# Two attention chunks per FFN group: the factor chain in one unit, the second chunk one unit up, gate work behind the output additions, one table preload

## Chip, cores, metric

One core of one Trainium2 chip runs the whole kernel. The metric is the time of one execution on the device in microseconds; the value for the kernel before is the median of three runs.

## What is computed

Two sequences of 1,024 tokens, 512 features, fp32. A gated linear attention with a state of 64 x 128, added to its input, then a ternary gated FFN, added again:

```python
x = L0_attn_x                                   # (2, 1024, 512)
x = x + attn(layernorm(x))
x = x + ffn(layernorm(x))

# attn: q,k (K=64), v (V=128) from projections
beta  = sigmoid(x @ Wb + bb);  delta = softplus(x @ Wd + bd)
S = beta_t[:, None] * S + delta_t[:, None] * outer(k_t, v_t)     # a scan over t
o_t = q_t @ S;   result = o @ Wo

# ffn: w1, w2 (1408 x 512), w3 (512 x 1408), quantised
quant(w) = clip(round(w / (mean(|w|) + 1e-8)), -1, 1)
hidden = sigmoid(x @ quant(w1).T) * (x @ quant(w2).T)
result = hidden @ quant(w3).T
```

## The kernel before

Each engine has its own program, in an order written out by hand; semaphores join them. Nothing is reordered: an instruction that waits holds everything behind it on its engine.

**Chunks.** The scan is cut into C = 8 chunks of 128 tokens, both sequences together. A first part of the kernel (up to about 74 us) loads everything, projects all chunks, and carries attention through for chunks 0 and 1. Gates (beta, delta and the key factor) are made there for chunks 0 to 3; those of chunks 4 to 7 come later, by `exps(c)` on ScalarE (L532 to L535: Abs, Exp, Exp, Ln), `gates(c)` on VectorE (L700 to L702) and `gates(c)` on GpSimd (L399 to L407).

**Attention of one chunk** (`attn(s, c)` on each engine, s is a stage): `fetch` on GpSimd (L418 to L423) spreads factors, 21 small operations; `chain0` and `chain1` on VectorE are the seven products of a chain (L741), 4 and 3 of them; `levels` on TensorE (L954 to L959) is 28 + 4 + 1 small fp32 matmuls that need the chain; `gt` on ScalarE (L569) copies one result; `masks` on VectorE (L766, L771) puts the scores together; `o` on TensorE (L967 to L973) needs the masks; `state` on VectorE (L777), `oT` on ScalarE (L574); `wo` on TensorE (L984), four matmuls; `resid` on VectorE (L784) adds to x; `norm2` (L679 on VectorE, L380 to L386 on GpSimd); `apply` (L796); `xhi` on ScalarE (L581), `xlo` on VectorE (L802) and GpSimd (L444) split the normed x in two fp16 parts; `turn_x` on SyncE's queue (L305) transposes them by DMA into `xT`.

**FFN.** G = 4 groups of two chunks, 512 tokens each. A group has UNITS = 15 units: units 0 to 10 each make one of the HT = 11 hidden tiles with 16 fp16 matmuls (L1058: eight for the gate, eight for the up product), units 11 to 14 are the DT = 4 down units of 22 matmuls (L1072). Behind unit u of the first kind come the sigmoid on ScalarE (L645), the product hid on VectorE (L870), its high part on ScalarE (L651) and low part on VectorE (L875). Behind a down unit comes the output addition y on VectorE (L886), then a store. Three PSUM banks rotate, so a matmul group n waits for the reader of group n - 3; the first two of a group of the FFN wait for the output additions y(2) and y(3) of the group before:

```python
if m < 0:
    if n < 2 and g > 0:
        pe.wait_ge(y_ready, g * DT - 1 + n)
```

**Where attention lies in the FFN.** In group g < 3 the two chunks 2g + 2 and 2g + 3 are computed between the units, by the tables `PE_AFTER`, `DVE_AFTER`, `ACT_AFTER`, `POOL_AFTER`: each stage has a pair, the unit for the first and for the second chunk. On VectorE stages come behind hid and the low part of a unit u < 11 and ahead of y in a unit u >= 11. Group 3 has no attention. In group 0 the weights are also made ternary: `round12`, `round3` on VectorE (L728, L735; tables `R12_AT`, `R3_AT`), `sign12`, `sign3` on ScalarE (L553, L562; `W12_AT`, `W3_AT`), and a DMA transpose of each tile on SyncE's queue (L311, L320), which also carries x's transposes and the stores, in order, with three slots each for the signed tiles. `EXPS_AT` and `GATES_AT` say behind which (group, unit) the late gates are made. ScalarE's sigmoid needs another function table than Exp and Ln.

Of the kernel before, what the change touches and what calls it, by code (L numbers as in the profile page):

```python
# [16 lines left out]
def build_gated_delta_ternary_ffn(nc, x, Wq, Wk, Wv, Wo, Wb, bb, Wd, bd, w1, w2, w3, out):  # L17
# [8 lines left out]
    G = C // 2  # L26
# [19 lines left out]
    with ctx:  # L46
# [17 lines left out]
        wo = sb("wo", [P, D])  # L64
# [31 lines left out]
        oT = sb("oT", [P, B, P])  # L96
# [60 lines left out]
        def kept(c, a, b):  # L157
            return store[:, c, a * P:b * P]
# [58 lines left out]
        def sums_at(which):  # L217
# [1 line left out]

        UNITS = HT + DT  # L220

        PE_AFTER = {"levels": (2, 8), "o": (4, 10), "wo": (5, 11)}
        DVE_AFTER = {"chain0": (0, 6), "chain1": (1, 7), "masks": (2, 8), "state": (4, 10),
                     "resid": (5, 11), "norm2": (5, 11), "apply": (6, 12), "xlo": (7, 13)}
        ACT_AFTER = {"gt": (2, 8), "oT": (4, 10), "xhi": (7, 12)}
        POOL_AFTER = {"fetch": (0, 3), "norm2": (6, 12), "xlo": (7, 13)}

        W12_FRONT = 3
        W12_AT = {0: (3, 4), 1: (5, 6), 2: (7, 8), 3: (9, 10)}
        W3_AT = {4: (0, 1), 5: (2, 3), 6: (4,), 8: (5, 6), 9: (7, 8), 10: (9, 10)}  # L230
        R12_AT = {0: (7, 8), 1: (9, 10)}
        R3_AT = {2: (0, 1), 3: (2, 3), 5: (4,), 6: (5,), 7: (6, 7)}
        EXPS_AT = {(0, 11): (4, 5), (0, 13): (6,), (1, 11): (7,)}
        GATES_AT = {(0, 12): (4,), (0, 13): (5,), (0, 14): (6,), (1, 11): (7,)}
        R3_CUT = (0, 5 * P, H)

        def stages(after, u):

            return [(s, k) for s in after for k in range(2) if after[s][k] == u]
# [110 lines left out]
        def _(pool):  # L350
# [77 lines left out]
            def norm2(c):  # L428
                pool.wait_ge(stats2_ready, c + 1)
                rstd(c, C + c, mv2, rs2, XS).then_inc(rstd2_ready, 1)  # L430
# [9 lines left out]
            def xlo(c):  # L440
                if c > 0:
                    pool.wait_ge(xT_in, 16 * B * c)
                pool.wait_ge(xhi_ready, B * c + 1)
                nc.gpsimd.tensor_tensor(xs[:, 0, 1, :], xn2[:, 0, :], xs[:, 0, 0, :],  # L444
                                        ALU.subtract).then_inc(xlo0_ready, 1)
# [28 lines left out]
            for g in range(1, G - 1):  # L474
                fetch(2 * g + 2)
                if g == 1:
                    gates(5)
                    gates(6)
                fetch(2 * g + 3)
                norm2(2 * g + 2)  # L480
                xlo(2 * g + 2)
                if g == 1:
                    gates(7)
                norm2(2 * g + 3)
                xlo(2 * g + 3)

        @block.scalar
        def _(act):
# [38 lines left out]
            def exps(c):  # L527
                s = scratch(c)
                act.wait_ge(z_copied, c + 1)
                if c > 1:  # L530
                    act.wait_ge(stored, c - 1)
                nc.scalar.activation(s.z_abs, kept(c, 2, 3), ACT.Abs, bias=bias[:, 1:2])  # L532
                link(nc.scalar.activation(s.e_b, kept(c, 3, 4), ACT.Exp, scale=-1.0, bias=bias[:, 0:1]))
                link(nc.scalar.activation(s.e_d, s.z_abs, ACT.Exp, scale=-1.0))
                nc.scalar.activation(s.z_ln, s.e_d, ACT.Ln, bias=ones[:, 0:1]).then_inc(z_ready, 1)  # L535
# [30 lines left out]
            def attn(s, c):  # L566
                if s == "gt":
                    act.wait_ge(levels_done, c + 1)
                    nc.scalar.activation(GT[:, :], gt_at, ACT.Copy).then_inc(gt_ready, 1)  # L569
                if s == "oT":  # L570
                    act.wait_ge(o_done, c + 1)
                    if c > 0:
                        act.wait_ge(attn_done, c)
                    nc.scalar.activation(oT[:, :, :], oc[:, :].rearrange("p (b n) -> p b n", b=B)[:, :, 0:P],  # L574
                                         ACT.Copy).then_inc(oT_ready, 1)
                if s == "xhi":
                    if c > 0:
                        act.wait_ge(xT_in, 16 * B * c)
                    for b in range(B):
                        act.wait_ge(xn2_ready, B * c + b + 1)  # L580
                        nc.scalar.activation(xs[:, b, 0, :], xn2[:, b, :], ACT.Copy).then_inc(xhi_ready, 1)  # L581
# [57 lines left out]
            def group(g):  # L639
                for u in range(UNITS):  # L640
                    if u < HT:
                        act.wait_ge(gate_done, g * HT + u + 1)
                        if g * HT + u > 1:
                            act.wait_ge(hid_ready, g * HT + u - 1)
                        nc.scalar.activation(sig[:, u % 2, :], bank[2 * u % 3][:, :], ACT.Sigmoid,  # L645
                                             scale=1.0 / XS).then_inc(sig_ready, 1)
                    if 1 <= u <= HT:
                        act.wait_ge(hid_ready, g * HT + u)
                        if u == 1 and g > 0:
                            act.wait_ge(down_done, g * DT)  # L650
                        nc.scalar.activation(hid[:, 0, u - 1, :], hid32[:, (u - 1) % 2, :],  # L651
                                             ACT.Copy).then_inc(hi_ready, 1)
                    for c in EXPS_AT.get((g, u), ()):
                        exps(c)
                    if g == 0:
                        for j in W12_AT.get(u, ()):
                            sign12(j)
                        for j in W3_AT.get(u, ()):
                            sign3(j)
                    if g < G - 1:  # L660
                        for s, k in stages(ACT_AFTER, u):
                            attn(s, 2 * g + 2 + k)

            for g in range(G):
                group(g)
# [2 lines left out]
        def _(dve):  # L668
# [28 lines left out]
            def gates(c):  # L697
                s = scratch(c)
                dve.wait_ge(z_ready, c + 1)
                nc.vector.tensor_scalar(s.u_1, s.e_d, 1.0, -1.0, ALU.add, ALU.add).then_inc(u_ready, 1)  # L700
                link(nc.vector.tensor_scalar(s.e_b, s.e_b, 1.0, None, ALU.add))
                nc.vector.reciprocal(kept(c, 3, 4), s.e_b).then_inc(beta_ready, 1)  # L702
# [159 lines left out]
            def group(g):  # L862
                for u in range(UNITS):
                    if u < HT:
                        dve.wait_ge(up_done, g * HT + u + 1)
                        dve.wait_ge(sig_ready, g * HT + u + 1)
                        if g * HT + u > 1:
                            dve.wait_ge(hi_ready, g * HT + u - 1)
                            dve.wait_ge(lo_ready, g * HT + u - 1)
                        nc.vector.scalar_tensor_tensor(hid32[:, u % 2, :], bank[(2 * u + 1) % 3][:, :],  # L870
                                                       HS / XS, sig[:, u % 2, :], ALU.mult,
                                                       ALU.mult).then_inc(hid_ready, 1)
                    if 1 <= u <= HT:
                        dve.wait_ge(hi_ready, g * HT + u)
                        nc.vector.tensor_tensor(hid[:, 1, u - 1, :], hid32[:, (u - 1) % 2, :],  # L875
                                                hid[:, 0, u - 1, :], ALU.subtract).then_inc(lo_ready, 1)
                    if u >= HT and g < G - 1:
                        for s, k in stages(DVE_AFTER, u):
                            attn(s, 2 * g + 2 + k)
                    for c in GATES_AT.get((g, u), ()):  # L880
                        gates(c)
                    if u >= HT:
                        m = u - HT
                        dve.wait_ge(down_done, g * DT + m + 1)
                        y = tile(2 * g + m // 2, m % 2)
                        nc.vector.scalar_tensor_tensor(y, bank[(2 * HT + m) % 3][:, :], 1.0 / HS, y, ALU.mult,  # L886
                                                       ALU.add).then_inc(y_ready, 1)
                    if u < HT and g < G - 1:
                        for s, k in stages(DVE_AFTER, u):
                            attn(s, 2 * g + 2 + k)  # L890
                    if g == 0:
                        for j in R12_AT.get(u, ()):
                            round12(j)
                        if u == 2:
                            steps(1)
                        for k in R3_AT.get(u, ()):
                            round3(k)
# [213 lines left out]
```

## Time and profile before

| | |
|---|---|
| median of 3 runs | 346.62 us (346.48 to 348.51) |
| the profiled execution | 346.52 us |
| its span, first to last instruction | 344.8 us |
| TensorE busy | 331.6 us |
| VectorE, ScalarE, GpSimd busy | 206.4, 148.4, 104.3 us |
| granted TensorE clock | 1.00 throughout |
| FFN of group 0, 1, 2, 3 begins at | 74.0, 144.4, 215.8, 284.4 us |

Times in the trace count from the span's first instruction. A matmul's shown duration overlaps with its successors', so busy and idle times of TensorE are to be read beside the starts. In a timeline row an "x16" is that many instructions merged, and the bracket gives the idle time of the engine ahead of the first and what ended it.

### The profile page before, as it was taken

The numbers are of one execution on the slowest core, as the hardware profiler recorded it, in microseconds if no ns is written. First come the engines' busy times: TensorE is split into PE (matmuls) and PEld (weight loads), VectorE is DVE, ScalarE is ACT, GpSimd is POOL, SyncE is SP. The second block draws the span as 40 slices with busy tenths as digits, with TensorE's granted clock in tenths as the row PEclk, the third lists the DMA queues.
The fourth block names the chain that finished last, engine by engine and source line by source line (L and its number), as shares of the span: only waits on it lengthen the run. The fifth ranks groups of instructions, "written<-read, shape, count | busy, mean of one in ns | idle before, by whom it ended". The sixth has DMA issues, their size and how long they took to land.

```text
span 344.8 us, 5204 instructions
## 1 busy us (share of the span) xinstructions
PE 331.6 (96%) x1826; PEld 184.1 (53%) x1826; DVE 206.4 (60%) x454; ACT 148.4 (43%) x276; POOL 104.3 (30%) x350
## 2 busy tenths in 40 slices
PE   8899999998999999989999999999999999999996
PEld 6788878864544544435445444455454444444442
DVE  3678999299959836467388454473884433242311
ACT  1588687789745484522332512123332011323200
POOL 5797545495004003991032027200210110000000
PEclk9999999999999999999999999999999999999999
DMA  8999600457540720500003004100030040000011
GB/s 234 353 390 403 239 0 2 93 96 139 104 92 16 108 46 30 124 31 2 0 0 63 0 25 117 43 1 3 0 62 2 30 122 32 0 0 3 0 61 61
DMA packets 45658, 26.94 MB, mean 78 GB/s; under 512 B 37568, under 2 KB 38080, under 8 KB 45632
## 3 DMA queue, kind: packets, MB, share of 16 engines
q1 hardware_dynamic: 45632, 26.62, 28.2%
q8 instruction: 14, 0.23, 0.3%
q14 instruction: 12, 0.10, 0.1%
HBM read 13.89 MB, written 4.19 MB: 52 GB/s over the span
## 4 chain that ended last, share of the span: by engine, by line
PE 63%; DVE 16%; POOL 9%; issue 6%; ACT 3%; DMA 2%; SPq 1%; DVEq 0%; POOLq 0%; ACTq 0%
PE ffn L1058 34%; PE ffn L1072 13%; DVE X L741 4%; PE lev L954 4%; PE lev L984 4%; PE ffn L923 2%; DVE w_nat L875 2%; POOL rs L381 2%; DVE w_nat L728 2%; PE oc L970 1%; DVE x_sb L784 1%; DVE xn L796 1%; DVE stats L679 1%; DVE xnT L870 1%; DMA w_nat<-xs 1%
## 5 line engine op out<-in xcount | busy, mean ns | idle before, releaser
L1058 PE MATMUL ffn<-w_nat,w12T 128*128 128x512 f16 x704 | 154.9, 379 | 3.2 <-DVE x_sb L886 1.6
L1058 PEld LDWEIGHTS ffn<-w_nat,w12T 128*128 128x128 f16 x704 | 68.7, 98 | 85.9 <-DMA w_nat<-xs 2.3
L1072 PE MATMUL ffn<-w3T,w_nat 128*128 128x512 f16 x352 | 77.3, 379 | 0.2 <-DMA w3T<-xn 0.2
L645 ACT ACTIVATE xnT<-ffn 128x512 f32<-128x512 f32 x44 | 26.2, 596 | 91.8 <-PE ffn L1058 91.8
L870 DVE SCALAR_TENSOR_TENSOR xnT<-ffn,xnT 128x512 f32<-128x512 f32 x44 | 30.3, 690 | 56.8 <-PE ffn L1058 56.7
L1072 PEld LDWEIGHTS ffn<-w3T,w_nat 128*128 128x128 f16 x352 | 34.2, 98 | 42.7 <-issue 2.9
L380 POOL TENSOR_TENSOR ve<-mv,rconst 128x2 f32<-128x2 f32 x16 | 3.6, 222 | 121.2 <-DVE mv L683 121.2
L875 DVE TENSOR_TENSOR w_nat<-xnT,w_nat 128x512 f16<-128x512 f32 x44 | 32.3, 734 | 0.8 <-ACT w_nat L651 0.7
L651 ACT ACTIVATE w_nat<-xnT 128x512 f16<-128x512 f32 x44 | 27.4, 622 | 1.3 <-DVE xnT L870 1.3
L886 DVE SCALAR_TENSOR_TENSOR x_sb<-ffn,x_sb 128x512 f32<-128x512 f32 x16 | 10.7, 669 | 22.9 <-PE ffn L1072 22.9
L766 DVE COPY_PREDICATED sc<-mask,lev 128x128 f32<-128x128 uint32 x56 | 18.9, 338 | 5.7 <-PE oc L959 4.1
L679 DVE BATCH_NORM_STATS2 stats<-x_sb 128x6 f32<-128x512 f32 x32 | 20.5, 682 | 2.0 <-issue 1.7
L581 ACT ACTIVATE xs<-xn 128x512 f16<-128x512 f32 x16 | 9.2, 623 | 27.7 <-DVE xn L796 27.7
L784 DVE TENSOR_TENSOR x_sb<-x_sb,lev 128x512 f32<-128x512 f32 x14 | 9.0, 684 | 16.9 <-PE lev L984 16.9
L741 DVE TENSOR_TENSOR X<-X,tmk 128x256 f32<-128x256 f32 x42 | 18.2, 433 | 1.2
L923 PE MATMUL ffn<-xnT,wqk 128*128 128x256 f32 x64 | 15.5, 385 | 1.1 <-ACT xnT L505 0.8
L933 PE MATMUL pd<-wv,xnT 128*128 128x128 f32 x128 | 15.6, 275 | 0.0
L933 PEld LDWEIGHTS pd<-wv,xnT 128*128 128x128 f32 x128 | 15.1, 192 | 0.5 <-issue 0.5
L923 PE MATMUL ffn<-xnT,wbd 128*128 128x256 f32 x64 | 15.1, 379 | 0.0
L553 ACT ACTIVATE q<-w_nat,unround 128x512 f16<-128x512 f32 x22 | 14.2, 712 | 0.0
L444 POOL TENSOR_TENSOR xs<-xn,xs 128x512 f16<-128x512 f32 x8 | 9.3, 1157 | 14.9 <-ACT xs L581 14.9
L923 PEld LDWEIGHTS ffn<-xnT,wqk 128*128 128x128 f32 x64 | 11.7, 191 | 3.5 <-issue 2.3
(119 smaller groups left out, 387.4 us busy)
## 6 DMA issues: line engine op xcount, KB each, us to landing
x_sb<-in_L_attn_x_dram SPq DMA_DIRECT2D x16, 256.0 KB, 7.4
out_dram<-x_sb SPq DMA_DIRECT2D x16, 256.0 KB, 2.0
w_nat<-in_L_ffn_w_dram SPq DMA_DIRECT2D x2, 1536.0 KB, 11.1
w_nat<-in_L_ffn_w_dram SPq DMA_DIRECT2D x2, 1408.0 KB, 14.4
w_nat<-in_L_ffn_w_dram SPq DMA_DIRECT2D x2, 1280.0 KB, 12.2
wv<-in_L_attn_Wv_dram SPq DMA_DIRECT2D x1, 256.0 KB, 4.9
wo<-in_L_attn_Wo_dram SPq DMA_DIRECT2D x1, 256.0 KB, 14.2
w_nat<-xs SPq DMA_TRANSPOSE x16, 3.2
```

The source lines that it names most:

```text
L553: done = nc.scalar.activation(q12[:, j % QS, n, :], nat[n][:, j * D:(j + 1) * D], ACT.Sign, bias=unround[:, 0:1])
L645: nc.scalar.activation(sig[:, u % 2, :], bank[2 * u % 3][:, :], ACT.Sigmoid, scale=1.0 / XS).then_inc(sig_ready, 1)
L651: nc.scalar.activation(hid[:, 0, u - 1, :], hid32[:, (u - 1) % 2, :], ACT.Copy).then_inc(hi_ready, 1)
L679: done = nc.vector.bn_stats(stats[:, c, b, :], tile(c, b))
L741: step = nc.vector.tensor_tensor(FG(c, l + 1).rearrange("p (n h) -> p n h", h=h), FG(c, l).rearrange("p (n h) -> p n h", h=h), factors(c, ...
L766: link(nc.vector.copy_predicated(sc[:, :, :].rearrange("p b (n two h) -> p b n two h", two=2, h=h)[:, :, :, 1, :], level(mask[:, l, :], l) ...
L870: nc.vector.scalar_tensor_tensor(hid32[:, u % 2, :], bank[(2 * u + 1) % 3][:, :], HS / XS, sig[:, u % 2, :], ALU.mult, ALU.mult).then_inc( ...
L875: nc.vector.tensor_tensor(hid[:, 1, u - 1, :], hid32[:, (u - 1) % 2, :], hid[:, 0, u - 1, :], ALU.subtract).then_inc(lo_ready, 1)
L923: done = nc.tensor.matmul(z_bank(c)[:, a * 256:(a + 1) * 256], w[:, t, :], turned(c)[:, t, :, :], start=t == 0, stop=t == DT - 1)
L933: done = nc.tensor.matmul(pd[:, b * V:(b + 1) * V], turned(c)[:, t, b, :], wv[:, t, :], start=t == 0, stop=t == DT - 1)
L1058: done = nc.tensor.matmul(bank[n % 3][:, :], w12T[:, a * DT + t, u * P:(u + 1) * P], xT[:, g, part, t, :], start=t == 0 and part == 0, sto ...
L1072: done = nc.tensor.matmul(bank[(2 * HT + m) % 3][:, :], hid[:, part, j, m * P:(m + 1) * P], w3T[:, j, :], start=part == 0 and j == 0, stop ...
```

## The change

Nine edits to tables and order; no arithmetic is changed. chain1 of both chunks goes into chain0's unit (0 and 5 instead of 1 and 7). The second chunk's levels, masks, gt go from unit 8 to 7, o, state, oT from 10 to 9, wo from 11 to 10, chain0 from 6 to 5; resid, norm2 on VectorE and apply stay in 11, 11 and 12; GpSimd's norm2 goes from 12 to 11 (an order, no time), xlo from 13 to 12. Signing of w3 goes up by one unit from tile 5 on, rounding of w3 up by one or two. On GpSimd gates(7) goes behind both norms and xlos of group 2's x. On ScalarE the attention stages come ahead of signing and of exps, and a preload of a table set that holds both Exp and Ln comes ahead of the exps of (0, 11) and (1, 12). On VectorE the late gates of a unit come behind its output addition, and exps and gates get new places.

```diff
-        PE_AFTER = {"levels": (2, 8), "o": (4, 10), "wo": (5, 11)}
-        DVE_AFTER = {"chain0": (0, 6), "chain1": (1, 7), "masks": (2, 8), "state": (4, 10),
-                     "resid": (5, 11), "norm2": (5, 11), "apply": (6, 12), "xlo": (7, 13)}
-        ACT_AFTER = {"gt": (2, 8), "oT": (4, 10), "xhi": (7, 12)}
-        POOL_AFTER = {"fetch": (0, 3), "norm2": (6, 12), "xlo": (7, 13)}
+        PE_AFTER = {"levels": (2, 7), "o": (4, 9), "wo": (5, 10)}
+        DVE_AFTER = {"chain0": (0, 5), "chain1": (0, 5), "masks": (2, 7), "state": (4, 9),
+                     "resid": (5, 11), "norm2": (5, 11), "apply": (6, 12), "xlo": (7, 12)}
+        ACT_AFTER = {"gt": (2, 7), "oT": (4, 9), "xhi": (7, 12)}
+        POOL_AFTER = {"fetch": (0, 3), "norm2": (6, 11), "xlo": (7, 12)}
...
-        W3_AT = {4: (0, 1), 5: (2, 3), 6: (4,), 8: (5, 6), 9: (7, 8), 10: (9, 10)}
+        W3_AT = {4: (0, 1), 5: (2, 3), 6: (4,), 7: (5, 6), 8: (7, 8), 9: (9, 10)}
         R12_AT = {0: (7, 8), 1: (9, 10)}
-        R3_AT = {2: (0, 1), 3: (2, 3), 5: (4,), 6: (5,), 7: (6, 7)}
-        EXPS_AT = {(0, 11): (4, 5), (0, 13): (6,), (1, 11): (7,)}
-        GATES_AT = {(0, 12): (4,), (0, 13): (5,), (0, 14): (6,), (1, 11): (7,)}
+        R3_AT = {2: (0, 1), 3: (2, 3), 4: (4, 5), 6: (6, 7)}
+        EXPS_AT = {(0, 11): (4, 5), (0, 13): (6,), (1, 12): (7,)}
+        GATES_AT = {(0, 11): (4,), (0, 12): (5,), (0, 14): (6,), (1, 13): (7,)}
@@ gpsimd, groups 1 and 2
                 norm2(2 * g + 2)
                 xlo(2 * g + 2)
+                norm2(2 * g + 3)
+                xlo(2 * g + 3)
                 if g == 1:
                     gates(7)
-                norm2(2 * g + 3)
-                xlo(2 * g + 3)
@@ scalar, in a unit
-                    for c in EXPS_AT.get((g, u), ()):
-                        exps(c)
+                    if g < G - 1:
+                        for s, k in stages(ACT_AFTER, u):
+                            attn(s, 2 * g + 2 + k)
                     if g == 0:
                         for j in W12_AT.get(u, ()):
                             sign12(j)
                         for j in W3_AT.get(u, ()):
                             sign3(j)
-                    if g < G - 1:
-                        for s, k in stages(ACT_AFTER, u):
-                            attn(s, 2 * g + 2 + k)
+                    if (g, u) in ((0, 11), (1, 12)):
+                        nc.scalar.preload_act_table_set("natural_log_exp_and_others")
+                    for c in EXPS_AT.get((g, u), ()):
+                        exps(c)
@@ vector, in a unit
-                    for c in GATES_AT.get((g, u), ()):
-                        gates(c)
                     if u >= HT:
                         m = u - HT
                         dve.wait_ge(down_done, g * DT + m + 1)
                         y = tile(2 * g + m // 2, m % 2)
                         nc.vector.scalar_tensor_tensor(y, bank[(2 * HT + m) % 3][:, :], 1.0 / HS, y, ALU.mult,
                                                        ALU.add).then_inc(y_ready, 1)
+                    for c in GATES_AT.get((g, u), ()):
+                        gates(c)
```

## Rows read from the trace of the kernel before

**Rows 1.** The page, its first part: busy time and share by engine.
```profile
PE 331.6 (96%) x1826; PEld 184.1 (53%) x1826; DVE 206.4 (60%) x454; ACT 148.4 (43%) x276; POOL 104.3 (30%) x350
```

**Rows 2.** TensorE's waits from 80 us on: total us, times, longest.
```profile
PE lev L954 <- DVE X L741: 3.0, 4, 1.2
PE ffn L1058 <- DVE x_sb L886: 1.6, 1, 1.6
PE ffn L1058 <- DMA w_nat<-xs: 0.7, 1, 0.7
```

**Rows 3.** TensorE's timeline, group 0 and the first units of group 1: start, us.
```profile
81.08 3.61 PE L1058 MATMUL ffn<-w_nat,w12T 128*128 128x512 f16 x16
85.84 0.44 PE L954 MATMUL lev<-store 64*128 64x64 f32 x4 [1.15 <-DVE X L741]
...
123.31 2.33 PE L1072 MATMUL ffn<-w3T,w_nat 128*128 128x512 f16 x10
125.86 2.75 PE L1072 MATMUL ffn<-w3T,w_nat 128*128 128x512 f16 x12 [0.22 <-DMA w3T<-xn]
128.45 1.88 PE L984 MATMUL lev<-wo,oT 128*128 128x512 f32 x4
130.17 14.41 PE L1072 MATMUL ffn<-w3T,w_nat 128*128 128x512 f16 x66
144.41 1.89 PE L1058 MATMUL ffn<-w_nat,w12T 128*128 128x512 f16 x8
147.88 8.81 PE L1058 MATMUL ffn<-w_nat,w12T 128*128 128x512 f16 x40 [1.58 <-DVE x_sb L886]
156.62 0.44 PE L954 MATMUL lev<-store 64*128 64x64 f32 x4
...
158.77 7.07 PE L1058 MATMUL ffn<-w_nat,w12T 128*128 128x512 f16 x32
```

**Rows 4.** TensorE's timeline, second chunk of group 1 and start of group 2.
```profile
172.38 10.52 PE L1058 MATMUL ffn<-w_nat,w12T 128*128 128x512 f16 x48
183.54 0.44 PE L954 MATMUL lev<-store 64*128 64x64 f32 x4 [0.63 <-DVE X L741]
...
200.60 14.41 PE L1072 MATMUL ffn<-w3T,w_nat 128*128 128x512 f16 x66
215.76 4.49 PE L1058 MATMUL ffn<-w_nat,w12T 128*128 128x512 f16 x20 [0.75 <-DMA w_nat<-xs]
```

**Rows 5.** VectorE's timeline, group 0.
```profile
81.67 1.67 DVE L728 TENSOR_SCALAR w_nat<-w_nat,inv 128x512 f32<-128x512 f32 x4
...
84.45 1.33 DVE L741 TENSOR_TENSOR X<-X,tmk 128x256 f32<-128x256 f32 x3
...
135.45 1.00 DVE L796 TENSOR_SCALAR xn<-x_sb,mv,rs 128x512 f32<-128x512 f32 x2 [1.62 <-POOL rs L386]
...
147.20 0.63 DVE L886 SCALAR_TENSOR_TENSOR x_sb<-ffn,x_sb 128x512 f32<-128x512 f32 x1
```

**Rows 6.** Groups by line from 74 us on: count, busy us, mean ns.
```profile
L875 DVE TENSOR_TENSOR w_nat<-xnT,w_nat 128x512 f16<-128x512 f32 x44 | 32.3, 734 | 0.8 <-ACT w_nat L651 0.7
...
L422 POOL COPY tmk<-tot 128x32 f32<-128x32 f32 (+5 forms) x36 | 8.5, 235 | 0.0
...
L533 ACT ACT_TABLE_LOAD x4 | 5.1, 1283 | 0.0
```

**Rows 7.** One stretch: its us, then busy PE, PEld, DVE, ACT, POOL (counts).
```profile
96.50:118.50 22.00, 21.40 (x118) 10.53 (x119) 18.08 (x40) 11.02 (x21) 3.83 (x7) 1.00 0.41 64
```

**Rows 8.** The line of w3's transposes: ns min/median/max, and landing.
```profile
L320 SPq DMA_TRANSPOSE w3T<-xn x11: 1188/1264/1675, 95.7 to 123.2; - x11
...
DMA to landing us min/median/max: 2.4/2.5/3.2
```

**Rows 9.** Timelines of VectorE and GpSimd at one moment of group 1.
```profile
180.63 1.60 DVE L875 TENSOR_TENSOR w_nat<-xnT,w_nat 128x512 f16<-128x512 f32 x1
...
180.53 1.16 POOL L444 TENSOR_TENSOR xs<-xn,xs 128x512 f16<-128x512 f32 x1 [2.31 <-ACT xs L581]
```

## The prediction

> **What bounds the kernel now.** I read the page's busy line first [rows 1]: TensorE is busy for 96% of the span, VectorE for 60%. No other engine can be the bound on average, so the question is only where TensorE stands still, and whether the change removes that or makes new stands. The list of what TensorE waited for, from 80 us (the FFN) on, gives the whole answer [rows 2]: the factor chain on VectorE (L741) ahead of the level products, an output addition (L886) at a group's start, and the transposed x. That is 3.0 + 1.6 + 0.7 us; the reader should see that it is little, 1.5% of the time, and that hardly anything else can be won in the FFN, which has the same 1,056 matmuls before and after.
>
> The busy and idle columns understate a stall, since each matmul is shown for 0.38 us while the next starts much sooner. The pitch from start to start comes from 66 matmuls in a row that wait for nothing: (14.41 - 0.38) / 65 = 0.2158 us [rows 3]. A unit u < 11 (16 matmuls) is 3.45 us, a down unit (22) is 4.75. With it each stall is the real start less the start that the pitch gives [rows 3, 4]:
> - a: level products of chunk 2 in group 0. Unit 2 starts at 81.08 and ends at 84.53; an unhindered handover costs 0.11 (147.88 + 40 x 0.2158 = 156.51, levels at 156.62). They begin at 85.84: 1.20 us lost.
> - b: levels of the second chunk of a group. 172.38 + 48 x 0.2158 + 0.11 = 182.85, real start 183.54: 0.69. It is there three times (groups 0, 1 and 2; the waits list has four stands of 3.0 us together, the longest 1.2, so the other three are alike), so 2.07.
> - c: unit 11 of group 0. 123.31 + 4.75 = 128.06, next work at 128.45: 0.39, waiting for the transposed w3.
> - d: start of group 1. 144.41 + 8 x 0.2158 = 146.14, the ninth matmul at 147.88: 1.74, for the output addition.
> - e: start of group 2. 200.60 + 66 x 0.2158 = 214.84, real start 215.76: 0.92, for the transposed x.
>
> Sum 6.32 us. The idle figures of the same stands make only 5.5 (3.0 + 1.6 + 0.7 + 0.22). The Trainium skill (Perfetto Trace Analysis, opening note) calls matmul busy time a bad metric because matmuls are pipelined; by busy time alone the forecast would be 341.1. The trace agrees with the note: idle before 147.88 is shown as 1.58, the starts say 1.74.
>
> **The change, part by part.**
> 1. Chain whole in one unit. Nothing is added or removed; three products (1.33 us, L741) move ahead of two pairs of roundings (1.67 us at 81.67) and of the gate product of unit 1 behind them [rows 5]. For chunk 2 the chain ends at 81.67 + 1.33 = 83.0 instead of 85.8, so stall a goes: -1.20. What is delayed is hid(1): it ends near 85.2 instead of 83.9. Its reader on TensorE is the gate matmul of unit 3, which starts one set of level products (156.62 to 158.77: 2.15 us [rows 3]) after 84.6, at 86.8. So 1.6 us of cover; beyond that every further delay would be paid in full. Two roundings of w1/w2 slip by the same 1.3 us, with units of time before their matmuls. In groups 1 and 2 that chain ran without a stall and still does.
> 2. Second chunk up a unit. Chain in unit 5 whole, levels after unit 7 and no longer 8. The chain is then done some 4 us ahead of the levels: -2.07 for b. The wo products (1.72 us [rows 3], 128.45 to 130.17) go in front of unit 11; the same work. What is late next is VectorE's row of work between the end of o(2) and o(3), which needs the masks. In the window that holds it VectorE is busy for 18.1 us [rows 7]; xlo, hid and low part, three operations like L875 at 0.73 [rows 6] or 2.2, now come behind the masks, leaving 15.9. To that come two waits. One is for the end of unit 5: 3.45 less what lies before it, the state update (an estimate, two halves of L875) and two roundings (a half more than the 0.42 of L728's narrower ones [rows 5]), together 2.0, so 1.5. The other is for GpSimd's norm2, which no longer has a chain as cover: 1.62 in unit 12 behind an addition of 0.6 [rows 5]; here hid and low part, 1.4, cover part, so 0.8. Total 18.2 us, against TensorE's 5 x 3.45 + 1.72 + 2.15 = 21.1. Cover: 2.9 us in group 0, a little over that in groups 1 and 2, which have no roundings. Taken as nothing, bounded by 0 and 1 us for group 0.
> 3. ScalarE. GT and oT go before the sign work of the unit, so a ScalarE that waits for the level products has two to four sign operations queued behind it, and on SP's queue their transposes. In unit 2 this costs sign12(7), (8) about 2 us; units 7 and 8 use them more than 12 us later. On SP, the x transposes of chunk 2 (waiting for xlo, now behind the masks) come ahead of w3(7) to (10). Each issue holds the queue for 1.26 us and lands 2.5 us after it [rows 8]; three slots rotate. From xlo(2) near 116 two x transposes and w3(7) to (9) put the issue of w3(10) near 121.5 and its landing near 124; TensorE reads it at 123.3 + 10 x 0.2158 = 125.5. Now it is signed a unit later and gives stall c: -0.39, with 1.5 us of cover.
> 4. Gates behind the output additions. At the end of group 0 the addition y(3) stands behind gates(6), which hung on a chain of GpSimd and ScalarE work, and ran at 147.20 [rows 5]. Behind the change y(3) waits only for its matmuls. The gate of unit 0 takes 1.73 us before the up product needs that bank; the addition takes 0.63. d goes whole: -1.74. The gates (6) then run beside unit 0 of group 1, whose chain of chunk 4 needs only gates(4), done two units before; behind them on VectorE waits hid(0), whose reader on TensorE is the gate matmul of unit 2, one unit (3.45 us) later.
> 5. GpSimd's gates(7) behind the last xlo, and VectorE's xlo a unit sooner. x for group 2 landed late because its norm stood behind gates(7); now xlo(5) is done in unit 12, two down units (9.5 us) before the group starts. e goes: -0.92. The next fetch stands behind gates(7), which wait for y(2) of unit 13; its 21 operations of 0.24 us at most [rows 6] take under 5 us from about 209 and end before the chain of unit 0 of group 2, some 4 us into a group that starts near 210.
> 6. One preload. Four exps have two table loads each now, of 1.28 us [rows 6] (the line shown is that of Exp, four loads; Ln has as many); two preloads remain. That takes 8 x 1.28 - 2 x 1.28 = 7.7 us from ScalarE, none of it on TensorE's path once part 4 holds: 0. If the preload failed to spare any load, the two exps of unit 11 would end 5.1 us later, and their gates stand behind additions of down units of 4.75 us each: still 0.
>
> Sum: 346.52 (profiled execution; span 344.8 and 1.7 around it) - 6.32 = 340.20. That execution is 0.10 below the median of 346.62, so the forecast for the median is 340.3 us. Under 1%, 3.5 us, a measurement of this kernel can't well be told from no change; the forecast lies beyond.
>
> **The rivals.**
> - R1, the cover of parts 2 or 3 is short: VectorE is late with the masks, or w3(10) with its transposes behind x. Against: 2.9 and 1.5 us of cover. For: L875 stretched from 0.73 on average [rows 6] to 1.60 while GpSimd's xlo of 1.16 ran beside it [rows 9], and that xlo now meets the same gate pair and the masks. One such meeting costs 0.9, inside the cover; two and a slow norm2 bring stands of 0.5 to 2.5 us in all: 340.8 to 342.8.
> - R2, the group starts stay: something else is the last releaser at d and e, for instance x of the next group landing after xlo, or gates that still reach the addition. Then a, b and c go (3.66) and 2.66 stay: 343.0; with half of b lost as well, 344.
> - R3, slower: VectorE falls a unit behind in units 5 to 9 of every group. The mechanism is the stretch just named, from 0.73 to 1.60, applied to all the VectorE operations with two SBUF inputs there: 7 chain products (3.1 us by 1.33 for three [rows 5]) grow by 3.7 and five L875 by 4.4, 8.1 in all, less 2.9 of cover: 5.2 x 3 = 15.6, less 6.32: 356. The Trainium skill (GPSIMD Engine Reference, Specifications) says that GpSimd shares its SBUF interfaces with VectorE and contends with instructions of two SBUF inputs; taken at every instruction, it would give that time, and no row here has it at every one. Against: GpSimd is busy for only 3.8 of the 22 us [rows 7], which scales 8.1 to 1.4, under the cover. It decides from 2.1 us of new stands a group on (6.32 / 3), and 3.3 for over 1% slower.
>
> **How the numbers follow.** Forecast with its parts as worked out: 0.62 (339.7 to 340.8). R1: 0.17. R2: 0.17, of which 0.05 is below 343.1, the bound of 1%. R3: 0.04. Faster 0.62 + 0.17 + 0.05 = 0.84, same 0.12, slower 0.04. The range leaves out R3 and the upper part of R2 and reaches 0.8 under the forecast for a handover or two that gets cheaper: 339.5 to 343.0.
>
> **What would show it.** In the profile of the changed kernel the list of TensorE's waits from 80 us on should be nearly empty; levels of chunk 2 should start at 84.6, group 1 at 142.1 (144.41 - a - b - c), group 2 at 210.1, group 3 at 278.1, the last matmul about 335. A line L954 <- L741 says that part 1 or 2 failed; a masks line (L766) before L967 or w3T before L1072 is R1; L886 or x's transposes at a group's start is R2; an L870 before L1058 in units 6 to 10 of all groups is R3. ScalarE should show two table loads for exps. The prediction is wrong if TensorE stands anywhere for over 2.5 us in all, or if the pitch isn't 0.216 any more.

## The result, and the profile after

| | before | changed |
|---|---|---|
| median (8 runs each) | 347.9 us (346.48 to 348.99) | 342.45 us (341.65 to 344.35) |
| ratio | | 0.986 (0.984 to 0.989) |
| profiled execution, span | 346.52, 344.8 us | 343.95, 342.2 us |
| FFN begins at | 74.02 us | 77.81 us |
| FFN: from there to the start of its last 88 down matmuls | 322.42 - 74.02 = 248.40 us | 319.88 - 77.81 = 242.07 us |

The change makes the kernel faster by 1.4%, where 1.8% was forecast. The last two lines hold the whole matter: the FFN lost 6.33 us, the sum of the prediction was 6.32; but the part ahead of the FFN, of which the change touches no line, is longer.

In some executions of either kernel TensorE's mean granted clock is 0.995 instead of 0.998 to 1.0 and the time about 1.5 us longer: four of the 8 of the kernel before, judged by their times (348.51 to 348.99), and two of the 8 of the changed one, the profiled one among them; the six others took 341.65 to 342.61, still 1.4 to 2.3 above the forecast of 340.3.

TensorE's waits from 74 us on in the changed kernel are a single one, and it stands at the FFN's start, where the kernel before has it too (0.82 at 74.02). From 80 us on, the stretch of [rows 2], none is left; the kernel before had the three kinds shown there and 0.2 for w3:

```profile
PE ffn L1060 <- DMA w_nat<-xs: 0.9, 1, 0.9
```

Its timeline there (start, us) answers to [rows 3] and [rows 4]:

```profile
77.81 7.08 PE L1060 MATMUL ffn<-w_nat,w12T 128*128 128x512 f16 x32 [0.87 <-DMA w_nat<-xs]
...
84.86 3.61 PE L1060 MATMUL ffn<-w_nat,w12T 128*128 128x512 f16 x16
88.41 0.44 PE L956 MATMUL lev<-store 64*128 64x64 f32 x4
...
126.94 19.16 PE L1074 MATMUL ffn<-w3T,w_nat 128*128 128x512 f16 x88
145.93 10.52 PE L1060 MATMUL ffn<-w_nat,w12T 128*128 128x512 f16 x48
...
172.15 7.07 PE L1060 MATMUL ffn<-w_nat,w12T 128*128 128x512 f16 x32
179.15 0.44 PE L956 MATMUL lev<-store 64*128 64x64 f32 x4
...
194.92 19.16 PE L1074 MATMUL ffn<-w3T,w_nat 128*128 128x512 f16 x88
213.91 10.52 PE L1060 MATMUL ffn<-w_nat,w12T 128*128 128x512 f16 x48
...
319.88 19.16 PE L1074 MATMUL ffn<-w3T,w_nat 128*128 128x512 f16 x88
```

No bracket of idle time is left behind the first row. The reader can lay the pitch of 0.2158 us to each pair: 84.86 + 16 x 0.2158 + 0.11 = 88.42 (a gone), 172.15 + 32 x 0.2158 + 0.11 = 179.17 (b gone), 88 matmuls from 126.94 to 145.93 in 18.99 (c gone) with 48 in a row behind them (d gone), the same 18.99 from 194.92 to 213.91 (e gone).

Ahead of the FFN the changed profile shows something else. First one stretch of the kernel before, then three of the changed one (columns as in [rows 7]; the last three numbers are the granted clock, the DMA engines' busy share and GB/s):

```profile
16.00:20.00 4.00, 3.87 (x26) 3.45 (x25) 0.97 (x4) 3.87 (x11) 3.50 (x9) 1.00 1.05 395
```
```profile
16.00:20.00 4.00, 3.87 (x30) 3.58 (x29) 0.55 (x1) 2.58 (x6) 3.42 (x10) 1.00 0.76 268
...
34.00:36.00 2.00, 2.00 (x25) 1.78 (x23) 0.70 (x1) 1.09 (x2) 1.57 (x7) 0.70 1.01 414
36.00:38.00 2.00, 2.00 (x7) 1.55 (x6) 1.74 (x5) 1.95 (x3) 2.00 (x14) 0.50 1.03 407
```

From 16 to 20 us the loads of x and the weights run at 268 instead of 395 GB/s. The four small bias loads are under way among them, and ScalarE's copy of the bias (L590) needs them. Its start, and the time of the loads from issue to landing, before and changed:

```profile
L590 ACT ACTIVATE bias<-bias x1: 204/204/204, 17.5 to 17.5; 128x1 f32<-128x1 f32 x1
...
DMA to landing us min/median/max: 7.3/7.8/8.5
```
```profile
L590 ACT ACTIVATE bias<-bias x1: 203/203/203, 20.4 to 20.4; 128x1 f32<-128x1 f32 x1
...
DMA to landing us min/median/max: 7.8/8.1/10.0
```

In this profile of the kernel before ScalarE does not wait for them. In the changed one it does (first view: total us, times, longest), and the last of the bias loads lies on the chain of work that leads to the FFN's start (second view: start and length, us):

```profile
ACT bias L590 <- DMA bias<-in_L_attn_bd_dram: 1.7, 1, 1.7
```
```profile
10.35 9.99 DMA bias<-in_L_attn_bd_dram
```

The copy is 2.9 us later, the gates and the chain of chunk 0 follow, and TensorE's first level products start at 33.23 behind a wait of 1.15 (before: 31.01 behind 0.41). From 34.8 us, 1.6 us behind the end of that wait, the granted clock is at half (1.2 GHz) for 3.4 us, and eight matmuls take 3.08 us there that take 1.89 otherwise:

```profile
33.23 0.44 PE L956 MATMUL lev<-store 64*128 64x64 f32 x4 [1.15 <-DVE X L743]
...
35.81 3.08 PE L925 MATMUL ffn<-xnT,wqk 128*128 128x256 f32 x8
38.73 1.89 PE L925 MATMUL ffn<-xnT,wbd 128*128 128x256 f32 x8
```

Late loads 2.2 us, and the rest, about 1.6, is what 3.4 us at half the clock cost: the 3.8 us by which the FFN begins later. The second part is not peculiar to the change: in 9 of the 23 runs of the kernel before, timed beside the next kernels, the mean granted clock is 0.995 too, though no profile shows where in them it was low.

### The profile page after: what moved, and what is told of

It is laid out like the page before. It is cut to its first block, busy times and chain, and to the rows that moved or that the text cites. A ratio compares the mean times of both kernels' runs of the same rounds, so it can differ in the third digit from the quotient of the medians.

```text
span 342.2 us, 5198 instructions
## 1 busy us (share of the span) xinstructions
PE 333.4 (97%) x1826; PEld 186.0 (54%) x1826; DVE 205.0 (60%) x454; ACT 140.8 (41%) x270; POOL 101.9 (30%) x350
## 4 chain that ended last, share of the span: by engine, by line
PE 83%; DMA 4%; POOL 4%; SPq 3%; DVE 3%; ACT 2%; issue 1%; POOLq 0%
PE ffn L1060 45%; PE ffn L1074 22%; PE lev L956 4%; PE lev L986 4%; DMA bias<-in_L_attn_bd_dram 3%; PE ffn L925 2%; PE oc L972 1%; SPq L265 1%; PE oc L969 1%; DMA w_nat<-xs 1%; DVE X L743 1%; PE lev L975 1%; PE oc L959 1%; POOL xs L444 1%; PE oc L961 1%
## 5 line engine op out<-in xcount | busy, mean ns | idle before, releaser
L877 DVE TENSOR_TENSOR w_nat<-xnT,w_nat 128x512 f16<-128x512 f32 x44 | 30.8, 701 | 0.4
L925 PE MATMUL ffn<-xnT,wqk 128*128 128x256 f32 x64 | 16.6, 406 | 1.0 <-ACT xnT L505 0.8
L925 PEld LDWEIGHTS ffn<-xnT,wqk 128*128 128x128 f32 x64 | 12.6, 207 | 3.6 <-issue 2.0
L986 PE MATMUL lev<-wo,oT 128*128 128x512 f32 x28 | 13.2, 595 | 0.0
```

The source lines that it names most:

```text
L925: done = nc.tensor.matmul(z_bank(c)[:, a * 256:(a + 1) * 256], w[:, t, :], turned(c)[:, t, :, :], start=t == 0, stop=t == DT - 1)
L986: done = nc.tensor.matmul(wo_bank(c, b)[:, :], oT[:, b, :], wo[:, :], start=True, stop=True)
```

## The experiments

In all of them "FFN" is the length as in the table. It repeats within 0.2 us from profile to profile (248.40, 248.27 and 248.21 in three of the kernel before), so one profile is enough for it; where the whole time matters, medians of 4 to 12 runs are given. The parts and the padded kernels ran once each.

**First question: is the longer part ahead of the FFN chance?** Two kernels unchanged, and both with one edit:

```diff
-            for b in range(B):                       # SyncE's queue, behind 14 loads (10 statements)
-                rows = slice(b * K, (b + 1) * K)
-                sp_.dma_start(bias[rows, 0:1], ...)
-                sp_.dma_start(bias[rows, 1:2], ...)
+            for b in range(B):                       # ScalarE's queue, at its start
+                rows = slice(b * K, (b + 1) * K)
+                act.dma_start(bias[rows, 0:1], ...)
+                act.dma_start(bias[rows, 1:2], ...)
```

> The changed kernel once more, text unchanged. In the first profile its FFN (first to last start of the FFN's stretch, the first L1060 matmul to the first of the last 88) took 242.07 us against 248.40 before, as forecast, but began 3.8 us later (77.8 against 74.0), behind a late landing of the bias loads and a stretch at half the clock. Theory T1, the part ahead of the FFN varies by chance in both kernels: FFN again 242.1, the ratio of the medians nearer to 0.982 (6.3 of 347). Rival T2, the change makes the part ahead of the FFN some 1.3 us longer for good: ratio near 0.986 again.

Measured: median 341.81 (340.81 to 345.2), ratio 0.986 (0.982 to 0.990); FFN 242.08, begins at 75.25.

> The kernel before, text unchanged, as a measure of chance. T1: its profile shows the FFN beginning anywhere from 74 to 78 us, FFN 248.4 long, ratio 1.000 within 0.003. T2: the FFN begins near 74 to 75 again, and more than 1 us sooner than that of the changed kernel of the same call.

Measured: 346.86 against 347.02 of the same kernel, ratio 0.999; FFN 248.27, begins at 75.27. By these two profiles alone it looked like chance, by the times it didn't.

> The changed kernel with the four bias loads issued from ScalarE's queue at the start, not from SyncE's behind ten others. Theory B: the bias landing (10.0 us after issue in the changed kernel's profile, 8.5 at most before) set the chain of chunk 0 and cost 2.2 us there; then the bias lands before 16 us, L590 never waits, the FFN begins by 75 and the median falls by about 1 to 1.5 us to 341, with less spread. Rival C: the loads were late by the load on the DMA rings, whatever queue, or the clock's fall is what matters: the same median within 0.5 us.

Measured: 340.54 (340.50 to 340.58), ratio 0.981 (0.978 to 0.983); bias landing 3.0 to 3.8 us after issue, FFN 242.07, begins at 74.44. All of theory B came true, the small spread too (four runs, mean granted clock 0.999 or 1.0). The rate of all loads from 16 to 20 us is 387 GB/s here, close to the 395 of the kernel before: with the four small loads on another queue, not only their landing is early, the large loads are back at full rate too.

> The same move of the four bias loads in the kernel before. Theory B: gains as much as in the changed kernel, about 1 us or somewhat less as its median FFN start seems earlier (75.4 against 76.4 by the spans): 346.8. Rival C: no difference. The distance between this and the changed kernel with the same move is 6.3 us by T1 (FFN only), 5 by T2.

Measured: 346.85, ratio 1.000 (0.998 to 1.002). Nothing gained: theory B holds in the changed kernel only. Between these two kernels, which differ by the change alone and have the bias out of the way, lie 6.31 us, as forecast. So something in the changed kernel made its bias loads late, and more than by chance.

**Second: the parts of the change, each alone in the kernel before.**

```diff
# chain_whole_only
-"chain1": (1, 7)
+"chain1": (0, 7)
# second_chunk_up_only
-PE_AFTER = {"levels": (2, 8), "o": (4, 10), "wo": (5, 11)}
+PE_AFTER = {"levels": (2, 7), "o": (4, 9), "wo": (5, 10)}
-"chain0": (0, 6), "chain1": (1, 7), "masks": (2, 8), "state": (4, 10)
+"chain0": (0, 5), "chain1": (1, 5), "masks": (2, 7), "state": (4, 9)
...
# tail_only
-EXPS_AT = {(0, 11): (4, 5), (0, 13): (6,), (1, 11): (7,)}
-GATES_AT = {(0, 12): (4,), (0, 13): (5,), (0, 14): (6,), (1, 11): (7,)}
+EXPS_AT = {(0, 11): (4, 5), (0, 13): (6,), (1, 12): (7,)}
+GATES_AT = {(0, 11): (4,), (0, 12): (5,), (0, 14): (6,), (1, 13): (7,)}
```

second_chunk_up_only also has gt, oT, W3_AT and R3_AT as in the changed kernel, and ScalarE's stages ahead of signing. tail_only has the rest of the change: EXPS_AT and GATES_AT, the additions ahead of the gates, gates(7) last, xlo at unit 12, GpSimd's norm2 at 11, and both preloads; only the first lines of its edit stand in the diff.

> Part 1 alone in the kernel before: chain1 of the first chunk in unit 0. My sum: stall a (1.20 us) goes, nothing else moves, so the FFN (first L1058 start to the start of the last 88 down matmuls) is 248.4 - 1.2 = 247.2 us. Rival: the product of unit 1, late by 1.3 us, holds the gate matmul of unit 3 and gives part back: over 247.5. Read beside it: when the pitch of the opening warm-up matmuls goes from 0.21 to 0.11 us (4.6 to 4.8 in three profiles of the kernel before, 7.2 to 7.6 in three of the changed one). If that is tied to what the change is, it shows in one of the parts; if it is chance, it falls either way.

Measured: FFN 247.15, so 1.25 less.

> Part 2 with part 3's order of ScalarE and its weights' tables, alone in the kernel before. My sum: b (2.07) and c (0.39) go, FFN 248.4 - 2.5 = 245.9. Rival R1: VectorE late with the masks or w3(10) late: a wait of L967 for L771 or of L1072 for w3T, FFN over 246.2.

Measured: FFN 243.27, so 5.13 less and not 2.5. Its waits, and VectorE's timeline at the end of group 0:

```profile
PE lev L954 <- DVE X L741: 1.1, 1, 1.1
PE ffn L1058 <- DMA w_nat<-xs: 0.8, 1, 0.8
```
```profile
124.78 1.28 DVE L784 TENSOR_TENSOR x_sb<-x_sb,lev 128x512 f32<-128x512 f32 x2
...
142.02 0.23 DVE L700 TENSOR_SCALAR w_nat<-w_nat 128x128 f32<-128x128 f32 x1 [2.58 <-ACT w_nat L535]
...
143.55 0.64 DVE L886 SCALAR_TENSOR_TENSOR x_sb<-ffn,x_sb 128x512 f32<-128x512 f32 x1
```

The waits at both group starts are gone as well, with the gates still ahead of the addition; the one wait of L954 left is a. The wo products before unit 11 let chunk 3's residual start at 124.78 instead of 130.37 (5.6 us sooner), and the norm, xlo, GpSimd's gates and ScalarE's exps of gates(6) follow 5.6 to 3.6 us sooner. The addition still waits for gates(6), but starts at 143.55 instead of 147.20 and ends at 144.2; group 1 begins at 143.30 and needs its bank 1.73 us later.

> Parts 4 to 6 alone: gates behind the output additions, GpSimd's gates(7) last, xlo a unit sooner, preload. My sum: d (1.74) and e (0.92) go, FFN 248.4 - 2.7 = 245.7. Rival R2: without the second chunk a unit up its xlo is not early enough, e stays in part: 246 to 246.7.

Measured: FFN 245.70, so 2.70 less, as expected. The three parts alone make 1.25 + 5.13 + 2.70 = 9.08, together 6.33: d and e (2.7) can be removed by either of two parts. In its whole time tail_only, the only one of the three with the preloads, has almost none of its gain: 346.51 us against 347.01 for the kernel before beside it, while second_chunk_up_only took 341.32 and chain_whole_only 345.71 (one run each). Its FFN begins at 76.72, theirs at 73.97 and 74.47. The pitch of the warm-up matmuls fell from 0.21 to 0.11 us at 6.0 us here and in chain_whole_only, and in other profiles anywhere from 4.4 to 7.6 us (7.6 in the first profile of the changed kernel, 4.4 in its third): it is not tied to the change.

> The changed kernel with the late gates again ahead of the output addition of their unit on VectorE, all else as changed. If the order of these two carries d: gates(6) in unit 14 of group 0 wait for ScalarE's exps, which wait for gates(4) on GpSimd (done near 136 in the changed profile's terms), so by the earlier exps they are ready before unit 14 ends and the addition is late by no more than 0.5 us: FFN 242.1 to 242.6. Rival: the order is what counts, d comes back with 1.7: 243.8.

```diff
-                    if u >= HT: ...                  # output addition
-                    for c in GATES_AT.get((g, u), ()): gates(c)
+                    for c in GATES_AT.get((g, u), ()): gates(c)
+                    if u >= HT: ...
```

Measured: FFN 242.07. With the rest in place the order of gates and addition is worth nothing.

**Third: how much cover does VectorE have?** Memsets that compute nothing, ahead of the second chunk's chain:

```diff
                 if s == "chain0":
+                    # c odd and over 2; N is 4 or 10
+                    for _ in range(N):
+                        link(nc.vector.memset(wqk[:, :, :], 0.0))
```

> The changed kernel with four linked memsets of 128x512 on VectorE ahead of the second chunk's chain in unit 5 of groups 0 to 2 (an estimate of 0.5 us each, 2.1 us a group, from the 0.91 us of the 128x1024 one); they compute nothing. It measures the cover of VectorE between o(2) and o(3), which I put at 2.9 us in group 0. If that holds, nothing is waited for and the FFN stays at 242.1. Rival: the cover is below 2 us; a wait of L969 for the masks (L768) appears in group 0 at least.

Measured: each memset with its link takes 0.66 us, 2.6 a group. FFN 245.11, 3.0 more, with these waits:

```profile
PE ffn L1063 <- DVE xnT L875: 1.5, 1, 1.5
PE ffn L1063 <- DMA w_nat<-xs: 0.9, 1, 0.9
PE oc L972 <- DVE sc L776: 0.8, 2, 0.4
PE ffn L1077 <- DMA w3T<-xn: 0.2, 1, 0.2
```

By the starts: in group 0 unit 9's gate product waits for hid(7) (1.66 us), in groups 1 and 2 o waits for the masks (0.5 each), so the cover there is some 2 us. In group 0 the added 2.6 us moved a meeting: two roundings ahead of hid(7) took 2.06 us beside GpSimd's xlo that take 1.14 in the changed kernel, 0.9 more. There the same xlo runs beside the low part behind hid(7), which takes 1.53 instead of 0.68. So hid(7) is late by 3.6 us and not by 2.6, and the masks behind both by little more than 2.6. The row c (w3) is back as well (0.40 by the starts). In the changed kernel itself the masks of group 0 are done 1.2 us ahead of o(3):

```profile
116.09 2.58 DVE L768 COPY_PREDICATED sc<-mask,lev 128x128 f32<-128x128 uint32 x7
118.70 0.44 DVE L773 COPY_PREDICATED sc<-ident,oc 128x256 f32<-128x256 uint32 x1
```

(118.70 + 0.44 = 119.1, o(3) starts at 120.32.) My 2.9 us was more than double of what there is, and the rival of the expectation came true.

> The same with ten memsets, about 5.2 us a group, 2.3 more than the 2.9 us of cover. If my sum is right TensorE stands about 2 us in group 0 and 1 to 2 in groups 1 and 2: FFN 246 to 248.5, about as long as before the change. Over 250 would say that the delay is paid more than once in a group, under 244 that the cover is 4 us or more.

Measured: FFN 261.71, 19.6 more for three times 6.6 us, and far above the 246 to 248.5 that I expected. TensorE's level products of the second chunk now wait for the residual of the first (L789) three times 3.7 us, and that isn't all:

```profile
PE lev L959 <- DVE x_sb L789: 11.2, 3, 3.7
```
```profile
110.00:115.00 5.00, 1.49 (x27) 1.52 (x28) 4.78 (x14) 0.00 (x0) 0.00 (x0) 1.00 0.00 0
115.00:119.00 4.00, 4.00 (x19) 1.84 (x17) 3.01 (x6) 2.06 (x4) 2.09 (x7) 0.57 0.00 0
...
187.00:194.00 7.00, 6.47 (x40) 4.67 (x41) 5.90 (x15) 1.94 (x4) 2.98 (x7) 0.52 0.00 1
```

With each stand of 3.7 us the granted clock goes to half, 1.7 us behind its end in group 0 and 0.7 and 0.3 us ahead of its end in groups 1 and 2, for 3.4, 6.8 and 6.8 us. If half of this time is lost (an estimate), that is 8.5 us; with the stands of 11.2 it makes the 19.6 within 0.1.

**Fourth: the preload.**

```diff
-                    if (g, u) in ((0, 11), (1, 12)):
-                        nc.scalar.preload_act_table_set("natural_log_exp_and_others")
```

> The changed kernel without the two preloads. Each exps should load two tables again (1.28 us each). My part 6 put the preload at nothing on TensorE's path: FFN 242.1 with 8 loads in exps. Rival: exps late, then gates late, then a wait at a group's start: over 242.5.

Measured: FFN 242.07, with eight loads in exps: on that path the preload is worth nothing. But the time of this single run was 340.43, bias landing 8.5 at most, FFN from 74.29. That made the preload a suspect for the part ahead of the FFN, 50 us and more before it runs.

> The changed kernel without its two preload lines, timed. Theory P: the preloads, 50 us and more behind, lengthen the part ahead of the FFN (later landing of the bias loads); without them the median is 340.5 (one look gave 340.43), some 1.3 us under the changed kernel's, bias copy (L590) near 18.0, FFN start 74 to 74.6. Rival Q, chance: median 341.8 to 342.4 like the changed kernel's, bias copy 19 or later.

Measured: 340.26 (340.13 to 340.71), ratio 0.982 (0.981 to 0.983); bias landing 8.5 at most, L590 at 17.7, FFN from 74.11.

> The changed kernel once more as the control of this call. Theory P: bias landing over 9 us, median 341.8 to 342.5. Rival Q: may come out at 340.5 as well.

Measured on the same chip: 343.31 (342.24 to 343.51), ratio 0.990 (0.989 to 0.991); landing 10.0, L590 at 19.9, the clock at half from 35.1 to 38.5, FFN 242.07 from 77.34. That is 3.05 us more than without the preloads, but two of these four runs, the profiled one among them, have a mean clock of 0.995. Over its three timings, on different chips, the changed kernel has twelve runs with a clock of 0.998 or more, 340.81 to 343.51 with a median of 342.2; without the preloads all five runs took 340.13 to 340.71. So the preloads cost about 2 us.

> The kernel before with the two preload lines ahead of exps in (0, 11) and (1, 11) and nothing else. Theory P: its FFN gets shorter by up to 1.7 us (exps spare 2.6 us ahead of y(3)), its part ahead of the FFN longer by 1 or more; bias landing at 9.3 us or more, L590 after 19. Rival Q: landing 8.3 to 8.5, L590 near 18, time below that of the kernel before by the FFN's gain.

Measured: 347.03, ratio 1.002 (1.000 to 1.004), with a FFN of 246.57, 1.8 less. L590 at 19.6, landing 9.4. The two lines alone shorten the FFN and lose all of it ahead of it. Here, where the gates still stand ahead of the addition, the preload is on TensorE's path: the wait of d is gone.

Rates of the loads from 16 to 20 us, without preloads (the changed kernel) and with them (the kernel before):

```profile
16.00:20.00 4.00, 3.87 (x26) 3.47 (x25) 0.95 (x4) 3.87 (x11) 3.47 (x9) 1.00 1.00 374
```
```profile
16.00:20.00 4.00, 3.87 (x27) 3.50 (x26) 0.55 (x1) 2.25 (x7) 3.42 (x10) 1.00 0.67 236
```

Theory P holds. Next, what it is about the preload:

> The changed kernel with the preload of (0, 11) alone; exps(7) load their two sets again as before the change. If the added instruction does it: rate in 16 to 20 us under 280 GB/s, bias landing over 9 us, median 342 or more. If it is that the separate Exp and Ln sets drop out of the program: rate 340 or more, landing 8.3 to 8.5, median 340.3.

Measured: 340.47 (340.18 to 340.91), ratio 0.980 (0.977 to 0.982); landing 8.2 at most, L590 at 17.5, 382 GB/s from 16 to 20 us. One added preload does no harm. With it in one place the program still loads the separate Exp and Ln sets for chunk 7:

```profile
L662 ACT ACT_TABLE_LOAD x1 | 1.3, 1283 | 0.0
L533 ACT ACT_TABLE_LOAD x1 | 1.3, 1283 | 0.0
L535 ACT ACT_TABLE_LOAD x1 | 1.3, 1283 | 0.0
```

**Fifth: a faster kernel.** The changed kernel with the bias loads on ScalarE's queue, and one step of the part ahead of the FFN moved:

```diff
+        def xs_of(c, b):
+            if c == 1:
+                return w12T[:, DT + b, 3 * P:H].rearrange("p (s n) -> p s n", s=2)
+            return xs[:, b, :, :]
...
             sign12(0)
             vcopy(5)
+            attn("xhi", 1)
             apply(7)
             zcopy(6)
             evacuate_T(7)
-            attn("xhi", 1)
```

> The changed kernel, bias loads on ScalarE's queue, and the split of chunk 1's normed x taken ahead of the last first norm on ScalarE, into a place of its own (w12T's columns for tiles 3 to 10, not written yet) so that it needn't wait for the transposes of chunk 0. In the profile of the own-queue kernel ScalarE stands 1.7 us ahead of apply(7) and the FFN waits 0.87 us for those transposes. If they set the FFN's start, it begins 0.87 us sooner and the time is 339.7 against 340.54. Rival: the transposes of the first weight tile, or the rounding on VectorE, hold the FFN's start or its first units as long: 340.5.

Measured: 339.90 (339.61 to 340.18), ratio 0.979 (0.976 to 0.981); the FFN begins at 73.47 with no wait and is 242.06 long: TensorE's list of waits from 74 us on is empty. Against 340.54 without the early split, on another chip, that is 0.64 less where 0.87 was expected.

> The fastest version so far (339.9: bias loads on ScalarE's queue, early split of chunk 1) without the two preload lines. If the preloads act through the bias landing alone, which here no longer matters, it is the same 339.9 within 0.3. If they act also through the opening (pitch of the warm-up matmuls), or otherwise, it is 339.5 or less.

Measured: 339.75 (339.61 to 339.91), ratio 0.980 (0.979 to 0.982), within 0.15 us of the other. With the bias on its own queue the preloads cost nothing that can be seen: their harm needs the bias loads in SyncE's queue. Both the landing and the rate of the loads are then as without preloads (388 and 390 GB/s from 16 to 20 us in these two), so no run separates them; the trace of the changed kernel shows the wait at the landing (1.7 us ahead of L590).

## Why the prediction was right and where it failed

The forecast for the FFN came true with its mechanism; the step that failed is part 6, which put the preloads at 0 on TensorE's path. They cost about 2 us ahead of the FFN.

- **Reading of the stalls (a to e).** Right: 6.32 us worked out from pitch and starts, 6.33 measured (6.1 to 6.3 with the other profiles of the kernel before); by the idle column it would have been 5.5. Counted from the FFN's start, groups 1, 2 and 3 begin where the prediction has them (68.1, 136.1 and 204.1 us behind it). The chain's part and the tail's, each taken alone, moved their stalls by what the list says (1.25 for 1.20, 2.70 for 2.66). That the sum agrees to 0.01 is luck.
- **Part 6, the step that failed.** The preload was costed at nothing, with the exps' readers named as cover. That is so in the FFN (242.07 with and without), and ScalarE did get its time back (busy 148.4 us before, 140.8 after, where 7.7 less were forecast). It was wrong for the program: with the two lines the bias loads in SyncE's queue landed at 10.0 instead of 8.5 us and the loads of the first 20 us were slower, which costs about 2 us in runs with a clock of 0.998 or more, and 3.05 in the medians on one chip (343.31 against 340.26). In the first result the median is 2.1 above the forecast (342.45 against 340.3). Why two lines at 126 us and later do this is open. I costed an edit by the place where its instruction stands, and the signs that I named all lie from 80 us on, because no line ahead of there changes; so none of them could show it.
- **Part 2, mis-sized.** The cover of 2.9 us is 1.2 at the masks: from o(2) to the masks' end VectorE is busy for 17.6 us and not 15.9, and idle for 2.5 where the two waits were put at 2.3. With GpSimd's xlo beside the roundings, hid(7) becomes the nearest reader. It did not decide, so the time is right for a reason that was weaker than stated. R1 was the rival that this touches; with 2.6 us more of VectorE's work it comes true.
- **Parts 4 and 5** took credit for d and e. They do remove them, but so does part 2 by itself, and with part 2 the order of addition and gates is worth nothing. What I missed is that moving wo ahead of unit 11 brings the residual 5.6 us and gates(6) with the addition behind them 3.6 us forward.
- **Part 3** held: w3 is not waited for, and in kernels with this part the wait came back only with 2.6 or 6.6 us of load on VectorE (0.2 and 0.3 by the idle column).
- **R3** needed VectorE a unit behind in every group. With 6.6 us added the time did go to 362.14; 8 to 9 of its 19.6 us came from a thing that was not in the rival, the clock behind a stand.
- **The number.** The range of 339.5 to 343.0 held the median of 342.45, and that is luck: its upper part was there for R1 and R2, and neither occurred. Two of the eight runs lie above it (343.95 and 344.35). The forecast of 340.3 is what the changed kernel does without its preloads (340.26) or with one (340.47).

## What to carry to other kernels

Work out a stall from starts and pitch, not from the idle column, and sum the stalls: that alone gave the FFN's gain within the 0.2 us by which its length repeats, where the idle column is 0.8 short. When an edit adds or removes a table set, or anything else that is part of the program as a whole, look at the loads at the kernel's start in the next profile, even if the edit stands far behind. Try a queue of its own for a small load that the first chain needs, instead of a place behind megabytes of x and weights: in the changed kernel it landed in 3.8 us instead of 9.3 to 10, and the spread of the run times went from 4.4 (six runs, two of them with a clock of 0.99 or 0.995) to 0.1 us (four runs). In the kernel before the same move gained nothing (346.85 against 347.02).

## What the runs showed of the hardware that I had not expected

- Landing of the last bias load, SyncE's queue: 8.2 to 8.5 us in seven profiles of kernels whose program uses the separate Exp and Ln table sets, 9.3 to 10.6 in eight of kernels whose every exps has the preload of the common set; rate of all loads from 16 to 20 us 340 to 395 against 236 to 273 GB/s. With the bias loads on ScalarE's queue the rate was 386 to 390 in four profiles, two of them with both preloads. Why is open: the number of sets and the program's layout change together, and no run tells these apart.
- After a stand of TensorE the granted clock can be at half (1.2 GHz): from 34.8 us for 3.4 us in the changed kernel, behind a wait of 1.15; for up to 6.8 us with one of 3.7. It was at half for 3.4 us, too, behind a wait of 1.16 in changed_third and one of 0.96 in changed_gates_before_y. The same wait of 1.15 in tail_only's profile, and one of 1.55 in changed_pad4's, had no such stretch; so the length of the wait alone doesn't decide. A stand of 3.7 us cost up to 7 in this way (an estimate: 3.7 and half of 6.8).
- At the kernel's start the warm-up matmuls went from a pitch of 0.21 to 0.11 us at some moment between 4.4 and 7.6 us in equal programs, which moves the first transposes by 1 us (9.4 to 10.5).
